# Attention: the running maximum read from the scores' own bank, softmax work on two tiles an instruction, no diagonal matrices

## The chip, the cores and the metric

One core of one Trainium2 chip runs the whole program. The metric is the time on the device in microseconds; each kernel is run several times and the median is compared. TensorE (PE) does matrix products, VectorE (DVE), ScalarE (ACT) and GpSimd (POOL) do element work, SyncE (SP) issues the transfers here. SBUF is the memory that all engines read; PSUM is the memory into which TensorE writes, in eight banks of 512 float32 columns.

## What is computed

A gated cross-attention block followed by a sparse feed-forward block, in float32:

```
# x (4, 256, 512), ctx (4, 1601, 512); 32 query heads, 8 key/value heads, head size 128
lat = layernorm(x)
kv  = concat([ctx, lat], axis=1)              # 1857 rows per batch
q   = rms_norm(lat @ Wq);  k = rms_norm(kv @ Wk);  v = kv @ Wv
p   = softmax(q @ k.T / sqrt(128))            # 4 query heads share one key/value head
x   = x + tanh(g_xattn) * ((p @ v) @ Wo)
x   = x + tanh(g_ffn) * ffn(layernorm(x))     # argmax of 32 picks the active rows
```

The change touches the attention loop alone: k, v, the scores, the softmax and the product with v.

## The kernel before

The program has four stages. `prepare` makes the queries, `attend` does the attention, `project` the product with Wo, `ffn` the rest. All products are made of three passes over values that are split into a rounded high part and the remaining low part (HI, LO), so that float32 accuracy comes from faster products.

`attend` runs 4 batches x 8 key/value heads = 32 rounds. A round has two halves (`h`), and a half 15 tiles (`t`): a tile is 128 rows of keys (65 in the last) against 512 query columns. For each tile: TensorE makes the scores in one of two banks of `pqk` ("qk"), ScalarE copies them to `sc` in SBUF, scaled by the key's norm `rk` ("copy", L729), VectorE takes the running maximum over tiles in `mx` ("max", L784 and L787). After 15 tiles TensorE transposes `mx` ("mt"), VectorE reduces it to 4 columns ("red", L790), multiplies an identity with them to get four diagonal matrices (`diag`, L767), and one product of ones with those spreads the maximum over all partitions in `pmax` ("mb", L647). Then, tile by tile again: subtract the maximum (VectorE, "sub", L798, already two tiles an instruction), exp in place (ScalarE, "exp", L732), round to the high part (ScalarE, "hi", L736), take the low part (VectorE, "lo", L802), add up the exps over tiles in `sm` (GpSimd, "sum", L855), and the product with V (TensorE, "pv", L656). The sums go the same way as the maximum: transposed ("dt"), reduced, inverted, made diagonal (L767), spread ("db", L670), multiplied in ("on", L820).

Beside this the K and V projections of the coming round (`pkv`, two banks used in turn; each chunk of 512 rows in three parts), the splitting of K and V, the transposes of V ("vt") and the norms of K ("kn" on TensorE into a bank `pss` of its own, "var" on VectorE L830, "pow" on GpSimd L861) are woven in.

The order of each engine's instructions is written by hand as numbers: every step has a place on an axis on which a tile is 1 and a round is 30, and each engine does its own steps in the order of their places. `LAG` is the distance from a tile's scores to its product with V. Who waits for whom is written out as semaphores: `wait_ge(sc_ok, ...)` and so on. What TensorE waits for before it overwrites a score bank is this line (L634):

```
pe.wait_ge(sc_ok, AHEAD + T - 1)      # the copy of the tile before the last
```

A bank of `pkv` is free when the step that used it before has been read (`wait_for_bank`).

## Time and profile before

| | before |
|---|---|
| median of 3 runs | 3674.18 us (3670.4 to 3681.19) |
| profiled execution, span | 3683.3 us; no other time is given for it |
| TensorE busy | 3184.8 us (86%), granted clock 0.952 |
| VectorE busy | 3152.2 us (86%) |
| ScalarE busy | 2121.6 us (58%) |
| GpSimd busy | 1668.6 us (45%) |
| attention loop | from about 260 to 3205 us |

Busy shares are over the whole span, with stages of different limits; the stages ahead of and behind the attention keep VectorE less busy, so a share of one stage says more. The profile is one execution on the one core.

### The profile page before, as it was taken

Reading aid. Unit: us, or ns where it says so; the run is one execution under the profiler, and the core shown is the slowest. Engines: PE = TensorE matmul, PEld = TensorE weight load, DVE = VectorE, ACT = ScalarE, POOL = GpSimd, SP = SyncE. Lnnn points to the kernel's source line nnn. Section 1 sums busy time; section 2 is a strip of 40 time slices with the busy share of each in tenths; the row PEclk is TensorE's granted clock in tenths of the full one; section 3 lists DMA queues with packets and bytes.
Section 4 is the critical chain, followed back from the end, with each engine's and each line's share of the span. In section 5 each row is a group of like instructions: output and inputs, shape, how many; then the busy total and the mean of one; then the engine's idle time right before and its main releaser. Section 6 shows DMA issues by size and latency. Waiting matters only on the chain. (4 is left out here: it accounts for less than half of the span.)

```text
span 3683.3 us, 52901 instructions
## 1 busy us (share of the span) xinstructions
PE 3184.8 (86%) x14138; PEld 2429.3 (66%) x14138; DVE 3152.2 (86%) x3890; ACT 2121.6 (58%) x3795; POOL 1668.6 (45%) x1175
## 2 busy tenths in 40 slices
PE   7978898889798988887989889878888888599699
PEld 5856666666476666665766666656666666277477
DVE  6856999999979999999799999988999999732666
ACT  3435666666656666666666666666666666431211
POOL 2322556555536555555455555544555555400000
PEclk9989999999999999999999999999999999799799
DMA  7870000000200000011000100110100000153400
GB/s 239 263 230 24 29 28 28 28 28 29 73 33 29 28 28 31 35 46 48 33 29 31 44 30 28 35 57 27 42 32 29 28 28 12 54 172 97 150 34 18
DMA packets 179314, 210.99 MB, mean 57 GB/s; under 512 B 10452, under 2 KB 125140, under 8 KB 174056
## 3 DMA queue, kind: packets, MB, share of 16 engines
q1 hardware_dynamic: 174408, 196.27, 16.2%
q0 software_dynamic: 2176, 8.39, 0.7%
q10 hardware_dynamic: 2592, 4.72, 0.4%
q8 instruction: 58, 0.95, 0.1%
q14 instruction: 80, 0.66, 0.1%
HBM read 140.14 MB, written 69.21 MB: 57 GB/s over the span
## 5 line engine op out<-in xcount | busy, mean ns | idle before, releaser
L855 POOL TENSOR_TENSOR att_sm<-att_sm,att_sc 128x512 f32<-128x512 f32 (+1 forms) x832 | 1305.6, 1569 | 545.9 <-ACT att_sc L732 490.1
L656 PE MATMUL att_ppv<-att_pr,att_V 128*128 128x512 f32 (+1 forms) x2880 | 907.6, 425 | 191.5 <-DVE att_pr L802 185.0
L732 ACT ACTIVATE att_sc<-att_sc 128x512 f32<-128x512 f32 (+1 forms) x960 | 611.9, 637 | 642.5 <-DVE att_sc L798 642.1
L802 DVE TENSOR_TENSOR att_pr<-att_sc,att_pr 128x512 fp32r<-128x512 f32 (+1 forms) x960 | 924.0, 964 | 0.7 <-ACT att_pr L736 0.7
L787 DVE TENSOR_TENSOR att_mx<-att_mx,att_sc 128x512 f32<-128x512 f32 (+1 forms) x832 | 883.6, 1062 | 41.2 <-ACT att_sc L729 38.5
L635 PE MATMUL att_pqk<-att_q,att_kT 128*128 128x512 f32 (+1 forms) x2880 | 881.3, 415 | 3.1 <-DVE att_kT L824 2.3
L605 PE MATMUL att_pkv<-att_ctxT,att_wkv 128*128 128x512 f32 (+1 forms) x3072 | 799.3, 384 | 75.9 <-DVE att_kT L824 71.8
L656 PEld LDWEIGHTS att_ppv<-att_pr,att_V 128*128 128x128 f32 (+1 forms) x2880 | 529.6, 198 | 421.4 <-DVE att_pr L802 318.0
L729 ACT ACTIVATE att_sc<-att_pqk,att_rk 128x512 f32<-128x512 f32 (+1 forms) x960 | 656.2, 684 | 129.1 <-PE att_pqk L635 123.8
L605 PEld LDWEIGHTS att_pkv<-att_ctxT,att_wkv 128*128 128x128 f32 x3072 | 564.0, 192 | 218.7 <-DVE att_kT L824 98.6
L736 ACT CAST att_pr<-att_sc 128x512 fp32r<-128x512 f32 (+1 forms) x960 | 599.3, 624 | 176.2 <-PE att_ppv L656 172.2
L798 DVE TENSOR_TENSOR att_sc<-att_sc,att_pmax 128x1024 f32<-128x1024 f32 (+1 forms) x512 | 584.6, 1142 | 58.1 <-PE att_pmax L647 58.1
L635 PEld LDWEIGHTS att_pqk<-att_q,att_kT 128*128 128x128 f32 (+1 forms) x2880 | 528.0, 189 | 143.1 <-issue 32.2
L861 POOL TENSOR_TENSOR att_rk<-att_var,att_mhalf 128x4 f32<-128x4 f32 (+1 forms) x128 | 174.4, 1363 | 562.0 <-DVE att_var L830 483.0
L852 POOL TENSOR_TENSOR att_sm<-att_sc 128x512 f32<-128x512 f32 x64 | 96.7, 1511 | 241.1 <-ACT att_sc L732 209.1
L1005 PE MATMUL out_po<-out_wo,out_o 128*128 128x512 f32 x768 | 180.2, 396 | 29.5 <-DVE out_wo L981 23.5
L291 PE MATMUL pre_pq<-pre_wq,pre_xT 128*128 128x512 f32 x768 | 195.2, 404 | 6.0 <-issue 6.0
L1005 PEld LDWEIGHTS out_po<-out_wo,out_o 128*128 128x128 f32 x768 | 146.2, 191 | 64.7 <-issue 21.9
L291 PEld LDWEIGHTS pre_pq<-pre_wq,pre_xT 128*128 128x128 f32 x768 | 141.6, 191 | 35.1 <-issue 6.4
L670 PE MATMUL att_pred<-att_diag,att_ones 128*128 128x512 f32 x128 | 84.9, 751 | 85.2 <-DVE att_diag L767 85.2
L237 POOL TENSOR_TENSOR pre_rq<-pre_ms,pre_mhalf 128x4 f32<-128x4 f32 x64 | 64.4, 1007 | 165.4 <-DVE pre_ms L349 165.4
L693 PEld LDWEIGHTS att_pss<-att_ones,att_sq 128*128 128x128 f32 (+1 forms) x960 | 122.1, 189 | 10.5 <-ACT att_sq L748 1.6
(129 smaller groups left out, 2697.2 us busy)
## 6 DMA issues: line engine op xcount, KB each, us to landing
q_scr<-pre_qT SPq DMA_DIRECT2D x128, 256.0 KB, 3.5
att_wkv<-kv_scr SPq DMA_DIRECT2D x32, 1024.0 KB, 4.8
att_q<-q_scr SPq DMA_DIRECT2D x64, 512.0 KB, 4.3
o_scr<-att_on SPq DMA_DIRECT2D x64, 256.0 KB, 2.0
out_oraw<-o_scr SPq DMA_DIRECT2D x64, 256.0 KB, 4.9
att_sc<-in_ctx SPq DMA_DIRECT2D x16, 768.0 KB, 4.6
pre_wq_raw<-in_L_xattn_Wq SPq DMA_DIRECT2D x8, 1024.0 KB, 6.8
kv_scr<-pre_kv SPq DMA_DIRECT2D x8, 1024.0 KB, 7.6
```

Source lines behind the costliest of these rows:

```text
L291: mm = pe.matmul(pq[:, t % 4], xT[:, xp, c, t * P:(t + 1) * P], wq[:, j, wp, c], start=(i == 0), stop=(i == 3 * KT - 1))
L605: mm = pe.matmul(bank, wkv[:, which, wp, t], ctxT[:, xp, t, a:z], start=(i == 0), stop=(i == len(terms) - 1))
L635: mm = pe.matmul(pqk[0:m, (h * NT + t) % 2], kT[:, kp, t * P:t * P + m], q[:, qp, h], start=(i == 0), stop=(i == 2))
L656: mm = pe.matmul(ppv[:], V[0:m, vp, t], pr[0:m, pp, (h * NT + t) % NP], start=(t == 0 and i == 0), stop=(t == NT - 1 and i == 2))
L729: act.activation(sc[0:m, s], pqk[0:m, s % 2], ACT.Copy, scale=rk[0:m, t:t + 1]).then_inc(sc_ok, 1)
L732: act.activation(sc[0:m, s], sc[0:m, s], ACT.Exp).then_inc(exp_ok, 1)
L736: act.copy(pr[0:m, HI, s % NP], sc[0:m, s]).then_inc(phi_ok, 1)
L787: dve.tensor_tensor(mx[0:m, h], mx[0:m, h], sc[0:m, s], ALU.max).then_inc(max_ok, 1)
L798: dve.tensor_tensor(sc[0:m, s:s + w], sc[0:m, s:s + w], pmax[0:m].unsqueeze(1).to_broadcast([m, w, HALF]), ALU.subtract).then_inc(sub_ok, w)
L802: dve.tensor_tensor(pr[0:m, LO, s % NP], sc[0:m, s], pr[0:m, HI, s % NP].bitcast(F32), ALU.subtract).then_inc(plo_ok, 1)
L855: pool.tensor_tensor(sm[0:m, h], sm[0:m, h], sc[0:m, s], ALU.add).then_inc(sum_ok, 1)
L1005: mm = pe.matmul(po[:, t], o[:, v % SL, op, h], wo[:, wp, e * HC + h], start=(e == 0 and h == 0 and p == 0), stop=(e == NE - 1 and h == HC ...
```

## The change

1. The running maximum (step "max") no longer reads `sc` but the scores' bank itself, and scales on the way: `scalar_tensor_tensor` of PSUM, the norm column and `mx`. It now has an instruction for the first tile too. It still follows ScalarE's copy, and TensorE's next scores but one wait for it (`max_ok`) in place of the copy (`sc_ok`).
2. "exp", "hi", "lo" and "sum" work on groups `GR` of two tiles; `pr` holds two groups of two in place of three tiles. GpSimd sums into two columns blocks (`sm[:, 0:2]`), with one "fold" at the end of a half. "sum" waits for the low parts of its own group (`plo_ok`) in place of the exps.
3. No `diag`: `spread` multiplies four columns, each broadcast to 128, with the identity, into quarters of the bank.
4. The norms of K use the banks of `pkv`, so a round has 16 uses of these in place of 12; `vraw` holds two chunks in place of all; the weights of K and of V are loaded apart.
5. `LAG` is 24 in place of 21.5, and the places of V's chunks and transposes, of "red", "dt" and of the loads move.

```diff
-    NP = 3
+    NP = 2
+    GR = [(t, min(t + 2, NT)) for t in range(0, NT, 2)]
-        vraw = sb("vraw", [P, NT * P])
+        vraw = sb("vraw", [P, 2, 512])
-        pr = sb("pr", [P, 2, NP, HALF], F32R)
-        sm = sb("sm", [P, NH, HALF])
+        pr = sb("pr", [P, 2, NP, 2, HALF], F32R)
+        sm = sb("sm", [P, 2, HALF])
-        diag = sb("diag", [P, 4, P])
-        pss = ps("pss", [P, 512])
...
-        LAG = 21.5
+        LAG = 24
-                if t % 2 == 0:
-                    steps += [(p + LAG - 4.3, "sub", h, t)]
-                steps += [(p + LAG - 3.14, "exp", h, t), (p + LAG - 2.3, "hi", h, t),
-                          (p + LAG - 1.63, "lo", h, t), (p + LAG, "pv", h, t)]
-                if t >= 1:
-                    steps += [(p + 1.18, "max", h, t), (p + LAG - 1.5, "sum", h, t)]
+            for g, (t, z) in enumerate(GR):
+                p = h * NT + t + LAG
+                steps += [(p - 4.3, "sub", h, g), (p - 3.2, "exp", h, g), (p - 2.4, "hi", h, g), (p - 1.6, "lo", h, g)]
+                if g >= 1:
+                    steps += [(p - 0.9, "sum", h, g)]
+            for t in range(NT):
+                steps += [(h * NT + t + 0.9, "max", h, t)]
...
-        for c, (k, v, vt) in enumerate(((-12.7, 1, 10.6), (-9, 4, 15.5), (-3.21, 6.63, 20.25), (-1.5, 11.35, 24.37))):
+        for c, (k, v, vt) in enumerate(((-12.7, 1, 12.6), (-9, 6, 16.6), (-3.21, 13, 20.6), (-1.5, 17.5, 24.6))):
...
-        steps += [(-17, "ldw", 0, 0)]
+        steps += [(-28, "ldwk", 0, 0), (-10.4, "ldwv", 0, 0)]
...
+                def spread(bank, col):
+                    for c in range(4):
+                        mm = pe.matmul(bank[:, c * P:(c + 1) * P], col[:, c:c + 1].to_broadcast([P, P]), ident[:],
+                                       start=True, stop=True)
+                    return mm
...
-                        pe.wait_ge(sc_ok, AHEAD + T - 1)
+                        pe.wait_ge(max_ok, AHEAD + T - 1)
...
-                        pe.wait_ge(diag_ok, AHEAD + u + 1)
+                        pe.wait_ge(red_ok, AHEAD + u + 1)
                         pe.wait_ge(sub_ok, AHEAD + NT * u)
-                        pe.matmul(pmax[:], ones[:], diag[:].rearrange("p c n -> p (c n)"),
-                                  start=True, stop=True).then_inc(mb_ps, 1)
+                        spread(pmax, red).then_inc(mb_ps, 1)
...
+                        wait_for_bank(n, dn, before, xb)
                         pe.wait_ge(ksq_ok, AHEAD + NC * n + t + 1)
-                            mm = pe.matmul(pss[0:rows(i), i:i + 1], sq[:, t % 2, (i % 4) * P:(i % 4) * P + rows(i)],
+                            mm = pe.matmul(pkv[0:rows(i), BANK["kn", t], i:i + 1], sq[:, t % 2, (i % 4) * P:(i % 4) * P + rows(i)],
...
-                            dve.tensor_tensor(mx[0:m, h], mx[0:m, h], sc[0:m, s], ALU.max).then_inc(max_ok, 1)
+                            dve.scalar_tensor_tensor(out=mx[0:m, h], in0=pqk[0:m, s % 2], scalar=rk[0:m, t:t + 1],
+                                                     in1=mx[0:m, h], op0=ALU.mult, op1=ALU.max).then_inc(max_ok, 1)
...
-                        diagonal(red).then_inc(diag_ok, 1)
...
-                        dve.wait_ge(phi_ok, AHEAD + T + 1)
-                        dve.tensor_tensor(pr[0:m, LO, s % NP], sc[0:m, s], pr[0:m, HI, s % NP].bitcast(F32),
-                                          ALU.subtract).then_inc(plo_ok, 1)
+                        dve.wait_ge(phi_ok, AHEAD + grouped(n, h, t))
+                        dve.tensor_tensor(pr[0:m, LO, t % NP, 0:w], sc[0:m, h, i:i + w], pr[0:m, HI, t % NP, 0:w].bitcast(F32),
+                                          ALU.subtract).then_inc(plo_ok, w)
...
-                        pool.wait_ge(exp_ok, AHEAD + T + 1)
+                        pool.wait_ge(plo_ok, AHEAD + grouped(n, h, t))
...
+                            pool.wait_ge(sum_ok, AHEAD + grouped(n, h, t - 1))
+                            pool.tensor_tensor(sm[0:m, 0:w], sm[0:m, 0:w], sc[0:m, h, i:i + w], ALU.add).then_inc(sum_ok, w)
+                    elif what == "fold":
+                        pool.wait_ge(sum_ok, AHEAD + NT * (u + 1))
+                        pool.tensor_tensor(sm[:, 0], sm[:, 0], sm[:, 1], ALU.add).then_inc(fold_ok, 1)
```

Three places show what the numbers do to the order in the loop over rounds. The first is TensorE around the spread of the first half's maximum (`att_pmax`), from the transposes of V's second chunk on; `att_pkv<-att_ctxT,att_wkv` are the projections, 512 columns a full chunk, 322 the last. Before:

```order
L633 REGISTER_ALU
L635 MATMUL att_pqk<-att_q,att_kT 128x512 [waits att_sc_ok]
L635 MATMUL att_pqk<-att_q,att_kT 128x512 x2
L620 ISA [waits att_vraw_ok]
L605 MATMUL att_pkv<-att_ctxT,att_wkv 128x512 [waits att_w_in]
L605 MATMUL att_pkv<-att_ctxT,att_wkv 128x512 x3
L650 REGISTER_ALU
L656 MATMUL att_ppv<-att_pr,att_V 128x512 [waits att_plo_ok]
L656 MATMUL att_ppv<-att_pr,att_V 128x512 x2
L645 REGISTER_ALU
L646 ISA [waits att_diag_ok]
L647 MATMUL att_pmax<-att_diag,att_ones 128x512 [waits att_sub_ok]
```

Now:

```order
L635 ISA [waits att_vraw_ok]
L611 MATMUL att_pkv<-att_ctxT,att_wkv 128x512 [waits att_wk_in]
L611 MATMUL att_pkv<-att_ctxT,att_wkv 128x512 x3
L611 MATMUL att_pkv<-att_ctxT,att_wkv 128x322 [waits att_wv_in,att_vlo_ok]
L611 MATMUL att_pkv<-att_ctxT,att_wkv 128x322 x3
L664 REGISTER_ALU
L670 MATMUL att_ppv<-att_pr,att_V 128x512 [waits att_plo_ok]
L670 MATMUL att_ppv<-att_pr,att_V 128x512 x2
L660 REGISTER_ALU
L661 REGISTER_ALU [waits att_red_ok]
L619 MATMUL att_pmax<-att_ident,att_red 128x128 [waits att_sub_ok]
L619 MATMUL att_pmax<-att_ident,att_red 128x128 x3
```

The last chunk of V (322 columns) now stands ahead of the spread and waits for `att_vlo_ok`, the low half of the V transpose that TensorE has made just before.

The second is VectorE at the same place: the low parts (`att_pr`), the maximum (`att_mx`), the low half of V, the last subtraction of a half (`att_sc`, 65 rows). Before:

```order
L801 REGISTER_ALU
L802 TENSOR_TENSOR att_pr<-att_sc,att_pr 128x512 [waits att_phi_ok]
L798 TENSOR_TENSOR att_sc<-att_sc,att_pmax 65x512
L789 REGISTER_ALU
L790 TENSOR_REDUCE att_red<-att_pred 128x4 [waits att_mt_ps]
L767 TENSOR_TENSOR att_diag<-att_ident,att_red 128x512 [waits att_db_ps,att_red_ok]
L801 REGISTER_ALU
L802 TENSOR_TENSOR att_pr<-att_sc,att_pr 128x512 [waits att_phi_ok]
L836 REGISTER_ALU
L837 TENSOR_TENSOR att_V<-att_pkv,att_V 128x512 [waits att_vhi_ok]
```

Now:

```order
L816 REGISTER_ALU
L817 TENSOR_TENSOR att_pr<-att_sc,att_pr 128x1024 [waits att_phi_ok]
L794 REGISTER_ALU
L795 REGISTER_ALU [waits att_sc_ok]
L800 SCALAR_TENSOR_TENSOR att_mx<-att_pqk,att_rk,att_mx 128x512 [waits att_max_ok]
L845 REGISTER_ALU
L846 TENSOR_TENSOR att_V<-att_pkv,att_V 128x512 [waits att_vhi_ok]
L811 TENSOR_TENSOR att_sc<-att_sc,att_pmax 65x512
```

The last subtraction stood ahead of the reduction of the next maximum, two places ahead of V's low half; now it stands behind the next maximum and V's low half, and the spread above waits for it.

The third is GpSimd where a half's sums end; L861 and L863 before, L875 and L877 now, are the powers for the K norms. Before:

```order
L855 TENSOR_TENSOR att_sm<-att_sm,att_sc 128x512 [waits att_sum_ok,att_exp_ok]
L858 REGISTER_ALU
L860 REGISTER_ALU [waits att_var_ok]
L861 TENSOR_TENSOR att_rk<-att_var,att_mhalf 128x2 [waits att_sc_ok]
L863 TENSOR_TENSOR att_rk<-att_var,att_mhalf 65x1
L849 REGISTER_ALU
L855 TENSOR_TENSOR att_sm<-att_sm,att_sc 65x512 [waits att_sum_ok,att_exp_ok]
L849 REGISTER_ALU
L851 ISA [waits att_exp_ok]
L852 TENSOR_TENSOR att_sm<-att_sc 128x512 [waits att_dt_ps]
```

Now:

```order
L874 REGISTER_ALU [waits att_var_ok]
L875 TENSOR_TENSOR att_rk<-att_var,att_mhalf 128x2 [waits att_max_ok]
L877 TENSOR_TENSOR att_rk<-att_var,att_mhalf 65x1
L860 REGISTER_ALU
L866 TENSOR_TENSOR att_sm<-att_sm,att_sc 128x1024 [waits att_sum_ok,att_plo_ok]
L860 REGISTER_ALU
L866 TENSOR_TENSOR att_sm<-att_sm,att_sc 65x512 [waits att_sum_ok,att_plo_ok]
L868 ISA
L869 TENSOR_TENSOR att_sm<-att_sm 128x512 [waits att_sum_ok]
L860 REGISTER_ALU
L862 REGISTER_ALU [waits att_plo_ok]
L863 TENSOR_TENSOR att_sm<-att_sc 128x1024 [waits att_dt_ps]
```

A sum takes two tiles, waits for `att_plo_ok` in place of `att_exp_ok`, and an instruction that folds the two blocks stands behind the last.

## Rows read from the trace of the kernel before

**Rows 1.** Busy time by stretch: four rounds in a batch, and its first round.

```profile
core 0: us, PE busy (x) PEld busy (x) DVE busy (x) ACT busy (x) POOL busy (x), PEclk, DMA share, GB/s
1126.00:1474.00 348.00, 309.36 (x1381) 236.27 (x1380) 335.58 (x396) 235.67 (x431) 200.85 (x133) 0.97 0.09 30
...
1027.00:1060.00 33.00, 32.52 (x155) 26.05 (x156) 16.73 (x28) 18.03 (x31) 2.63 (x3) 1.00 0.21 74
```

**Rows 2.** Timeline of the transfer queue: two loads of K and V weights, four rounds apart.

```profile
1126.03 0.35 SPq L567 DMA_DIRECT2D att_wkv<-kv_scr  x1
...
1474.32 0.35 SPq L567 DMA_DIRECT2D att_wkv<-kv_scr  x1
```

**Rows 3.** Waits from 500 to 3000 us: who waited for whom, total, times, longest.

```profile
ACT att_sc L732 <- DVE att_sc L798: 554.2, 315, 3.4
...
POOL att_rk L861 <- DVE att_var L830: 392.3, 84, 10.3
...
PE att_ppv L656 <- DVE att_pr L802: 147.3, 165, 2.4
```

**Rows 4.** Groups of VectorE's instructions by shape, 1126 to 1474 us: busy, mean ns.

```profile
L802 DVE TENSOR_TENSOR att_pr<-att_sc,att_pr 128x512 fp32r<-128x512 f32 x112 | 106.4, 950 | 0.0
L787 DVE TENSOR_TENSOR att_mx<-att_mx,att_sc 128x512 f32<-128x512 f32 x96 | 103.9, 1083 | 0.5
...
L767 DVE TENSOR_TENSOR att_diag<-att_ident,att_rden 128x512 f32<-128x512 f32 x8 | 12.7, 1591 | 0.6
L787 DVE TENSOR_TENSOR att_mx<-att_mx,att_sc 65x512 f32<-65x512 f32 x8 | 9.8, 1224 | 0.0
```

**Rows 5.** Timeline of VectorE and of GpSimd, 1543 to 1552 us: start, duration.

```profile
1543.83 1.21 DVE L798 TENSOR_TENSOR att_sc<-att_sc,att_pmax 128x1024 f32<-128x1024 f32 x1
1544.96 0.68 DVE L802 TENSOR_TENSOR att_pr<-att_sc,att_pr 128x512 fp32r<-128x512 f32 x1
1545.56 1.77 DVE L787 TENSOR_TENSOR att_mx<-att_mx,att_sc 128x512 f32<-128x512 f32 x1
1547.26 1.78 DVE L802 TENSOR_TENSOR att_pr<-att_sc,att_pr 128x512 fp32r<-128x512 f32 x1
...
1545.21 6.70 POOL L855 TENSOR_TENSOR att_sm<-att_sm,att_sc 128x512 f32<-128x512 f32 x4
```

**Rows 6.** Single lines over the whole run: duration ns min/median/max.

```profile
L358 DVE SCALAR_TENSOR_TENSOR pre_qT<-pre_ptr,pre_wcol,pre_qT x64: 743/745/751, 46.7 to 247.4; 128x512 fp32r<-128x512 f32 x64
...
L977 DVE TENSOR_TENSOR out_o<-out_oraw,out_o x32: 1217/1224/1227, 3213.0 to 3391.6; 128x1024 fp32r<-128x1024 f32 x32
...
L855 POOL TENSOR_TENSOR att_sm<-att_sm,att_sc x832: 1261/1558/3655, 337.7 to 3195.2; 128x512 f32<-128x512 f32 x154, 65x512 f32<-65x512 f32 x13
```

**Rows 7.** Timeline of TensorE in the first round of a batch.

```profile
1031.07 0.95 PE L693 MATMUL att_pss<-att_ones,att_sq 128*128 128x1 f32 x8
1031.88 0.94 PE L635 MATMUL att_pqk<-att_q,att_kT 128*128 128x512 f32 x3
...
1039.04 0.85 PE L635 MATMUL att_pqk<-att_q,att_kT 128*128 128x512 f32 x3
1039.73 1.10 PE L605 MATMUL att_pkv<-att_ctxT,att_wkv 128*128 128x512 f32 x4
1040.67 0.87 PE L635 MATMUL att_pqk<-att_q,att_kT 128*128 128x512 f32 x3
...
1055.19 1.02 PE L647 MATMUL att_pmax<-att_diag,att_ones 128*128 128x512 f32 x2
1055.65 1.25 PE L635 MATMUL att_pqk<-att_q,att_kT 128*128 128x512 f32 x3
...
1083.02 0.76 PE L605 MATMUL att_pkv<-att_ctxT,att_wkv 128*128 128x322 f32 x4
1083.62 0.87 PE L635 MATMUL att_pqk<-att_q,att_kT 128*65 128x512 f32 x3
```

**Rows 8.** Timeline of TensorE and ScalarE: a tile's scores and their copy.

```profile
1504.01 0.85 PE L635 MATMUL att_pqk<-att_q,att_kT 128*128 128x512 f32 x3
...
1505.03 0.69 ACT L729 ACTIVATE att_sc<-att_pqk,att_rk 128x512 f32<-128x512 f32 x1 [0.54 <-PE att_pqk L635]
```

More of the change, by code:

```diff
@@ L470, in attend @@
                    for d, what in ((0, "xt"), (0.26, "xhi"), (0.6, "xlo"))]
-        loads = [(12.89, "ldw", 0, 0), (12.89 + .1, "ldlat", 0, 0)]
-        loads += [(z - 1 + LAG - 1.5 + .1, "ldx", 0, i) for i, (a, z) in enumerate(XP)]
+        loads = [(2, "ldwk", 0, 0), (19.6, "ldwv", 0, 0), (19.7, "ldlat", 0, 0)]
+        loads += [(z - 1 + LAG - 0.5, "ldx", 0, i) for i, (a, z) in enumerate(XP)]
         def window(*parts):
@@ L483, in attend @@
         in_boundary = [x for x in loads if x[0] >= UT]
-        start_early = [x for x in early if x[1] != "ldw"]
+        start_early = [x for x in early if x[1] not in ("ldwk", "ldwv")]
         START = window((0, -2 * UT, loads), (0, 0, context), (0, UT - 3.33, start_early))
@@ L491, in attend @@
         TAIL = window((-1, -UT, late))
-        USES = [(dn, what, c) for dn, what, h, c in MIDDLE if what in ("k", "v", "vt") and h == 0]
+        USES = [(dn, what, c) for dn, what, h, c in MIDDLE if what in ("k", "v", "vt", "kn") and h == 0]
         BANK = {(what, c): i % 2 for i, (_, what, c) in enumerate(USES)}
-        assert len(USES) == 3 * NC
+        assert len(USES) == 4 * NC
         BANK.update({("xt", i): i % 2 for i in range(CT)})
@@ L531, in rounds, with grouped, maxima @@
             run(B * KVH, TAIL, [], last=True)
-        def sums(n, h, t):
-            return n * UT + (h * NT + max(t, 1) + 1)
+        def grouped(n, h, g):
+            return tiles(n, h, GR[g][1] - 1)
+        def maxima(u, t):
+            return u * NM + t + 1
         def tiles(n, h, t):
@@ L638, in step @@
                     elif what == "mt":
-                        pe.wait_ge(max_ok, AHEAD + (NT - 1) * (u + 1))
+                        pe.wait_ge(max_ok, AHEAD + maxima(u, NT - 1))
                         pe.wait_ge(on_ok, AHEAD + u - 1)
@@ L665, in step @@
                         for c in range(4):
-                            mm = pe.transpose(pred[:, c * P:(c + 1) * P], sm[:, h, c * P:(c + 1) * P], ident[:])
+                            mm = pe.transpose(pred[:, c * P:(c + 1) * P], sm[:, 0, c * P:(c + 1) * P], ident[:])
                         mm.then_inc(dt_ps, 1)
                     elif what == "db":
-                        pe.wait_ge(ddiag_ok, AHEAD + u + 1)
-                        pe.matmul(pred[:], ones[:], diag[:].rearrange("p c n -> p (c n)"),
-                                  start=True, stop=True).then_inc(db_ps, 1)
+                        pe.wait_ge(rden_ok, AHEAD + u + 1)
+                        spread(pred, rden).then_inc(db_ps, 1)
                     elif what == "xt":
@@ L807, in step @@
                         dve.wait_ge(den_ok, AHEAD + u + 1)
+                        dve.wait_ge(db_ps, AHEAD + u)
                         dve.reciprocal(rden[:], den[:]).then_inc(rden_ok, 1)
-                        dve.wait_ge(rden_ok, AHEAD + u + 1)
-                        if last and h == 1:
-                            dve.wait_ge(db_ps, AHEAD + u)
-                        else:
-                            dve.wait_ge(mb_ps, AHEAD + u + 2)
-                        diagonal(rden).then_inc(ddiag_ok, 1)
                     elif what == "on":
```

117 lines of the change are left out of this document (62 added, 55 removed).

## The prediction

> **What bounds the kernel now.** I read the busy time of each engine by stretch first. In four whole rounds of the attention loop VectorE is busy 335.6 of 348 us (96%) and TensorE 309.4 (89%), ScalarE 235.7, GpSimd 200.9 [rows 1]. A round (one head of keys and values, two halves of 15 tiles) is the distance between loads of its weights: four of them lie between 1126.03 and 1474.32, so 87.1 us each [rows 2]. In the round that opens a batch, where no softmax work of an earlier round is left, TensorE is busy 32.5 of 33 us and VectorE half of it [rows 1]: that is what the loop looks like when TensorE sets the pace.
>
> The waits say the same. Over 2500 us ScalarE's exp waits 554 us for VectorE's subtraction and TensorE's product with V waits 147 us for VectorE's low halves [rows 3]. VectorE is the bound.
>
> The groups of VectorE's instructions by shape show why it is so full. The 512-column low-half subtraction (L802) has a mean of 950 ns, the maximum (L787) 1083 [rows 4], though both take 0.68 us when nothing is in the way. The timeline shows what is: during 6.70 us of four back-to-back sums on GpSimd, instructions with both inputs in SBUF take 1.77 and 1.78 us, one after the other, that is 0.68 plus a wait of 1.1, and the subtraction of the maximum, one input of which is PSUM, takes its usual 1.21 [rows 5]. So what stretches VectorE is GpSimd's sums, and only for instructions with two SBUF inputs.
>
> **VectorE, part by part, for one round** (a quarter of the counts of [rows 4]).
> - Stretching now: L802 112 x (0.950 - 0.68) = 30.2; L787 96 x (1.083 - 0.68) = 38.7 and 8 x (1.224 - 0.68) = 4.4; the diagonal of the reciprocals 8 x (1.591 - 0.68) = 7.3. Sum 80.6 over four rounds, 20.2 a round.
> - The maximum reads PSUM and SBUF. No row shows it on this operand pair with GpSimd at work; the nearest are the scaled subtraction of the first stage (L358, PSUM and SBUF, 745 ns [rows 6]) and L798, which does not stretch. I take 0.745, so 28 x 0.065 more, and two more instructions a round (a tile now costs one each, also the first) at 0.60 from start to start [rows 5]: +3.0. If it stretched as L787 does now: +11 more.
> - The diagonals go: four a round, 0.61 each unstretched: -2.4.
> - Low halves in pairs: 1.22 us for 1024 columns (L977 [rows 6]), about 1.13 from start to start as L798 has it [rows 5], against 2 x 0.60: 14 x 0.07 = -1.0.
> - The low halves' own stretching: a sum now waits for the low halves of its own pair, so it starts when VectorE has just left the port, and the next low half stands about two tiles (5 us) later, behind two maxima and a subtraction that read PSUM. A sum of two tiles costs at most 2 x 1.26 = 2.5 us [rows 6]. It is over by then, unless an rsqrt (L861) is queued before it. I keep 3 of the 20.2.
> Busy 335.6 / 4 = 83.9, less 20.2, less 2.4, less 1.0, plus 3.0, plus 3: 66 us a round. VectorE stops being the bound.
>
> **TensorE, for one round.** Three 512-column products take 0.70 from start to start, four take 0.94, four of 322 columns 0.60 [rows 7]. 30 scores and 30 products with V: 60 x 0.70 = 42.0; K and V projections 18 x 0.94 + 6 x 0.60 = 20.5; norms 3 x 0.81 + 0.5, four spreads at 0.46, and eight groups of four transposes at no more than that each: 8.4. That is 70.9. A spread becomes four products of 128 columns in place of one of 512, each with its own weight load: the same columns, so I cost it at nothing; at worst it doubles, +1.8 a round. This is at the full clock; the granted mean is 0.97 in [rows 1], and half-speed pieces stretch products while TensorE is the bound: 73.
>
> TensorE's work isn't spread evenly: where K or V parts stand beside a tile it has 2.3 us a tile, elsewhere 1.4, and there VectorE's 1.8 (half of 1.13 + 1.13 + 2 x 0.67) decides. With two score banks neither can run more than about a tile ahead. Adding the busier engine over ten stretches of three tiles gives 73, with the clock 75.
>
> **New waits.** The score bank was free after ScalarE's copy; now the next scores but one wait for VectorE's maximum. From the start of the scores to the copy is 1.02 us [rows 8], copy 0.69, maximum 0.75, handoffs 0.1 each: 2.6 us before VectorE can do anything that stands behind this maximum, 3.3 with that next instruction. At five places TensorE waits for just that, after work of only 0.70 + 0.94 us; the first two stand in the order rows, the others follow from the places given to the steps. (1) V's last chunk waits for the low half of the V transpose, one maximum behind: 1.6. (2) The spread of the maximum waits for the last subtraction of the half before, which the larger LAG put behind one more maximum: 1.5. (3) The norm products, now in the projections' banks: chunk 3 waits for the raw V behind a copy, 1.0. (4) K's third chunk waits for a V low half that follows the norms: 1.0. (5) Smaller ones at the third V transpose and the first norm, 0.6 together. Sum 5.7, of which I let 1.2 be hidden where VectorE decides anyway: 4.5. Round: 75 + 4.5 = 79.5.
>
> ScalarE does the same columns in fewer instructions and GpSimd's sums keep their columns. I cost both at nothing: at 59 and 50 us a round [rows 1] they hide behind TensorE's 73, and without that cover a gain of ScalarE would still be none.
>
> **Sum.** 87.1 - 79.5 = 7.6 us a round. In each of four batches about 40 us already run at TensorE's pace (33 of them in [rows 1]), so 30 rounds count: 228. The pipeline is 2.5 tiles longer and drains four times, 2.5 x 79.5 / 30 = 6.6 us each if nothing fills it, 0 if all; I take 12. 3683.3 - 228 + 12 = 3467. The page gives no time for the profiled execution beside its span; the span is 9 us above the median of the three runs, 3674. So 3458; I say 3455.
>
> **Rivals.**
> - *The new waits are hidden* (20%). For it: now VectorE idles only 4%, so this queue order has been tolerant. Then a round is 73 to 75: 3683 - 30 x 13 + 5 - 9, about 3290 (3260 to 3320).
> - *The maximum becomes the pace* (20%). For it: TensorE can't go two tiles ahead without it, and each late low half on VectorE is passed on. The waits double to 10 and a round is 84.5: 3683 - 30 x 2.6 + 26 - 9 = 3620; more likely half way, 3540.
> - *Longer sums block the low halves* (5%), the one that ends slower. Place: GpSimd's queue behind L861, which waits 392 us over 2500 for the variances [rows 3], so sums pile up and run back to back. Price: the wait of 1.1 us beside a sum of 1.26 to 1.56 becomes about 2.2 beside two tiles; 16 low halves a round x 2.2 = 35, VectorE 63 + 35 = 98, a round 102: 3683 + 30 x 15 - 9, over 4100. It decides from a mean wait of (83.9 - 63) / 16 = 1.3 us, where VectorE is back where it is now. Against it: the sum's new wait for its own low half, and only one instruction in four, not two, can be hit. The Trainium skill (SBUF — State Buffer, Who interferes with whom) says that the pair of ports is held for a whole GpSimd instruction and the other engine blocks fully, and that one SBUF input never contends. The first half speaks against this change, whose sums are twice as long, and leads to this rival; the second is what L798 shows in [rows 5].
> - *Nothing changes* (3%): TensorE, 89% busy, is already nearly the pace. Against it: 32.5 of 33 us when it is.
>
> **How the numbers follow.** The likeliest case (52%) is 3400 to 3520. To hold 8 in 10 the range goes from the hidden waits to the maximum's pace: 3290 to 3600. A measurement can tell 0.3% (11 us) from no change. The three cases that are faster hold 0.92, no change 0.03, the blocked low halves 0.05.
>
> **What would show it.** Mean of the maximum about 0.75 us and never over 1; low halves of 1024 columns near 1.3; no stretch over 2.5. VectorE 80 to 84% busy in a round, TensorE over 90%; a round 79.5 us. TensorE waiting some 5 us a round, for the V low half, the last subtraction and the maximum. I am wrong if low halves show a mean above 2 us, if the maximum stretches, or if TensorE's wait for the maximum is the largest group.

## The result

The changed kernel takes 3753.8 us (median of 4 runs, 3746.1 to 3759.1) against 3672.3 for the kernel before in the same comparison (3668.0 to 3681.2): a ratio of 1.021, with a 95% interval of 1.0183 to 1.0238. It is 2.1% slower, where 6% faster was forecast, and lies outside the range.

The page of the changed kernel gives the engines over the whole span of 3751.9 us (busy us, share, instructions).

```profile
PE 3214.2 (86%) x14906; PEld 2532.9 (68%) x14906; DVE 2568.1 (68%) x3378; ACT 2044.9 (55%) x2899; POOL 1350.9 (36%) x791
```

VectorE did 584 us less work (3152 before), as foretold, and it bought nothing: TensorE is busy for about as long as before (3214 against 3185 us) in a longer span. The groups of VectorE and GpSimd by shape, 500 to 3000 us (busy, mean ns, idle time before), answer to [rows 4]:

```profile
L800 DVE SCALAR_TENSOR_TENSOR att_mx<-att_pqk,att_rk,att_mx 128x512 f32<-128x512 f32 x701 | 523.2, 746 | 259.9 <-ACT att_sc L742 256.5 <-issue 0.8
L817 DVE TENSOR_TENSOR att_pr<-att_sc,att_pr 128x1024 fp32r<-128x1024 f32 x377 | 473.1, 1255 | 101.6 <-ACT att_pr L753 101.5
...
L866 POOL TENSOR_TENSOR att_sm<-att_sm,att_sc 128x1024 f32<-128x1024 f32 x269 | 643.2, 2391 | 576.5 <-DVE att_pr L817 575.9 <-issue 0.6
```

The maximum costs 746 ns with GpSimd at work (1083 before), a low half of two tiles 1255 (950 for one before). The stretching is nearly gone: the maximum's longest instruction takes 754 ns, and single low halves still reach 2.94 us. What came in its place shows in the waits of the same 2500 us (engine, what it waited for, total, times, longest), which answer to [rows 3]:

```profile
ACT att_sc L742 <- PE att_pqk L650: 746.7, 484, 6.9
...
PE att_pkv L611 <- DVE att_V L846: 93.0, 51, 3.1
...
PE att_ppv L670 <- ACT att_oraw L757: 71.6, 51, 1.7
...
PE att_pmax L619 <- DVE att_sc L811: 46.2, 27, 3.9
PE att_pqk L650 <- DVE att_mx L800: 41.2, 80, 0.7
PE att_pkv L706 <- ACT att_vraw L770: 37.3, 27, 1.4
PE att_pkv L720 <- DVE att_kT L833: 31.2, 27, 1.3
```

ScalarE now waits 747 us for TensorE: TensorE is the pace. And TensorE, on which everything hangs, waits 320 us in six groups, none of them large, for VectorE and ScalarE, which have time to spare. There are about 27 rounds in the stretch, so a group with 27 times is one wait a round, 51 two, 80 three. TensorE had waited in the kernel before as well, 147 us for the low halves in [rows 3], and in the same view of it these:

```profile
PE att_pred L670 <- DVE att_diag L767: 68.3, 49, 3.7
PE att_pkv L605 <- DVE att_kT L824: 61.9, 48, 1.8
```

In the 2500 us it was idle for 312 us then (2188 busy) and is idle for 349 now (2151 busy): old waits went and new ones came, a few more than before.

One round, by the same two marks as in [rows 2] (start, duration), is 1350.81 - 1261.85 = 88.96 us, against 87.1 before and 79.5 forecast (the 28 rounds that lie within a batch have a mean of 89.0); under the marks the busy times in it (PE, PEld, DVE, ACT, POOL, then the granted clock), which answer to [rows 1]:

```profile
1261.85 0.35 SPq L571 DMA_DIRECT2D att_wkv<-kv_scr  x1
...
1350.81 0.34 SPq L571 DMA_DIRECT2D att_wkv<-kv_scr  x1
```

```profile
1261.85:1350.81 88.96, 76.76 (x371) 61.17 (x370) 65.13 (x83) 56.73 (x82) 39.62 (x22) 0.98 0.08 29
```

All waits of TensorE of half a microsecond or more in that round, from its timeline (in brackets the idle time before the group), with a few rows on what a spread costs:

```profile
1264.20 0.66 PE L720 MATMUL att_pkv<-att_ident,att_vraw 128*128 128x128 f32 x4 [1.14 <-DVE att_kT L833]
...
1274.12 0.95 PE L670 MATMUL att_ppv<-att_pr,att_V 128*128 128x512 f32 x3 [1.39 <-ACT att_oraw L757]
...
1277.62 0.96 PE L650 MATMUL att_pqk<-att_q,att_kT 128*128 128x512 f32 x3 [0.53 <-DVE att_mx L800]
...
1282.65 1.20 PE L611 MATMUL att_pkv<-att_ctxT,att_wkv 128*128 128x512 f32 x4 [1.45 <-DVE att_V L846]
...
1302.33 1.16 PE L619 MATMUL att_pmax<-att_ident,att_red 128*128 128x128 f32 x8 [1.44 <-DVE att_sc L811]
1303.24 0.94 PE L670 MATMUL att_ppv<-att_pr,att_V 128*128 128x512 f32 x3
1304.02 0.86 PE L650 MATMUL att_pqk<-att_q,att_kT 128*128 128x512 f32 x3
1306.27 0.72 PE L706 MATMUL att_pkv<-att_ones,att_sq 128*128 128x1 f32 x6 [1.39 <-ACT att_vraw L770]
...
1311.08 0.96 PE L650 MATMUL att_pqk<-att_q,att_kT 128*128 128x512 f32 x3 [0.50 <-DVE att_mx L800]
...
1316.08 0.86 PE L670 MATMUL att_ppv<-att_pr,att_V 65*128 65x512 f32 x3
1316.77 0.90 PE L650 MATMUL att_pqk<-att_q,att_kT 128*128 128x512 f32 x3
1319.13 0.96 PE L670 MATMUL att_ppv<-att_pr,att_V 128*128 128x512 f32 x3 [1.46 <-ACT att_oraw L757]
...
1325.37 0.97 PE L650 MATMUL att_pqk<-att_q,att_kT 128*128 128x512 f32 x3 [0.66 <-DVE att_mx L800]
...
1341.45 0.86 PE L611 MATMUL att_pkv<-att_ctxT,att_wkv 128*128 128x322 f32 x4 [2.19 <-DVE att_V L846]
```

Their sum is 12.2 us; the rest of the round, 76.8, is TensorE's work. The wait of 1.46 shows how one arises. ScalarE's timeline for it:

```profile
1317.92 0.69 ACT L742 ACTIVATE att_sc<-att_pqk,att_rk 128x512 f32<-128x512 f32 x1 [0.65 <-PE att_pqk L650]
1318.50 0.58 ACT L757 COPY att_oraw<-att_ppv 128x512 f32<-128x512 f32 x1
```

The scores start at 1316.77. ScalarE's queue has their copy next (1317.92), and only behind it the copy of the finished output, "oraw" (1318.50), though the last product of the output, started at 1316.08, had ended 1.5 us before; TensorE's next product with V needs that bank and starts at 1319.13. So a step that is ready is held by a step that stands ahead of it in the handwritten order and waits for TensorE's newest work. Seven of the ten waits, 10.5 us together, have this form: scores, their copy, perhaps their maximum, then the late step. The other three, 1.7 us, are TensorE's waits for the maximum itself. There the copy had ended 0.9 to 3.2 us before the maximum started, and what stood ahead of it was other work in VectorE's queue, each time with a subtraction of two tiles (1.2 us) in it. The pairs add to the longest wait too, 2.19. VectorE's timeline for it:

```profile
1338.92 1.21 DVE L817 TENSOR_TENSOR att_pr<-att_sc,att_pr 128x1024 fp32r<-128x1024 f32 x1
1340.06 0.74 DVE L800 SCALAR_TENSOR_TENSOR att_mx<-att_pqk,att_rk,att_mx 128x512 f32<-128x512 f32 x1
1340.72 0.68 DVE L846 TENSOR_TENSOR att_V<-att_pkv,att_V 128x512 fp32r<-128x512 f32 x1
```

The copy ended at 1339.53; the low half of two tiles held the maximum, and so V's low half, 0.5 us longer.

### The profile page after: what moved, and what is told of

It is laid out like the page before. It is cut to its first block and busy times, and to the rows that moved or that the text cites. A ratio compares the mean times of both kernels' runs of the same rounds, so it can differ in the third digit from the quotient of the medians.

```text
span 3751.9 us, 52506 instructions
## 1 busy us (share of the span) xinstructions
PE 3214.2 (86%) x14906; PEld 2532.9 (68%) x14906; DVE 2568.1 (68%) x3378; ACT 2044.9 (55%) x2899; POOL 1350.9 (36%) x791
## 5 line engine op out<-in xcount | busy, mean ns | idle before, releaser
L866 POOL TENSOR_TENSOR att_sm<-att_sm,att_sc 128x1024 f32<-128x1024 f32 (+1 forms) x384 | 847.9, 2208 | 784.9 <-DVE att_pr L817 784.3
L800 DVE SCALAR_TENSOR_TENSOR att_mx<-att_pqk,att_rk,att_mx 128x512 f32<-128x512 f32 (+1 forms) x896 | 668.6, 746 | 321.5 <-ACT att_sc L742 316.7
L817 DVE TENSOR_TENSOR att_pr<-att_sc,att_pr 128x1024 fp32r<-128x1024 f32 (+1 forms) x512 | 624.0, 1219 | 122.5 <-ACT att_pr L753 122.1
L753 ACT CAST att_pr<-att_sc 128x1024 fp32r<-128x1024 f32 (+1 forms) x512 | 509.3, 995 | 101.4 <-PE att_ppv L670 100.6
L747 ACT ACTIVATE att_sc<-att_sc 128x1024 f32<-128x1024 f32 (+1 forms) x512 | 512.9, 1002 | 32.2 <-DVE att_sc L811 32.0
L875 POOL TENSOR_TENSOR att_rk<-att_var,att_mhalf 128x4 f32<-128x4 f32 (+1 forms) x128 | 146.5, 1145 | 531.0 <-DVE att_var L839 411.9
L863 POOL TENSOR_TENSOR att_sm<-att_sc 128x1024 f32<-128x1024 f32 x64 | 153.1, 2393 | 418.5 <-PE att_pred L680 394.8
L833 DVE TENSOR_TENSOR att_kT<-att_pkv,att_kT 128x512 fp32r<-128x512 f32 (+1 forms) x128 | 82.1, 642 | 154.7 <-ACT att_sq L765 154.1
L706 PEld LDWEIGHTS att_pkv<-att_ones,att_sq 128*128 128x128 f32 (+1 forms) x960 | 121.4, 189 | 69.0 <-ACT att_vraw L770 58.0
L706 PE MATMUL att_pkv<-att_ones,att_sq 128*128 128x1 f32 (+1 forms) x960 | 115.3, 240 | 45.4 <-ACT att_vraw L770 44.1
```

Of the source, the lines that this page charges most:

```text
L747: act.activation(sc[0:m, h, i:i + z - a], sc[0:m, h, i:i + z - a], ACT.Exp).then_inc(exp_ok, z - a)
L753: act.copy(pr[0:m, HI, t % NP, 0:z - a], sc[0:m, h, i:i + z - a]).then_inc(phi_ok, z - a)
L800: dve.scalar_tensor_tensor(out=mx[0:m, h], in0=pqk[0:m, s % 2], scalar=rk[0:m, t:t + 1], in1=mx[0:m, h], op0=ALU.mult, op1=ALU.max).then_i ...
L817: dve.tensor_tensor(pr[0:m, LO, t % NP, 0:w], sc[0:m, h, i:i + w], pr[0:m, HI, t % NP, 0:w].bitcast(F32), ALU.subtract).then_inc(plo_ok, w)
L866: pool.tensor_tensor(sm[0:m, 0:w], sm[0:m, 0:w], sc[0:m, h, i:i + w], ALU.add).then_inc(sum_ok, w)
```

## The experiments

Theory A: TensorE is the pace, and each of these waits is lost time of its own, so taking one away gives its size in each of some 32 rounds. Theory B: the score bank, held until VectorE's maximum, is what sets the pace. Theory C: the sums of two tiles hurt the low halves after all. The median follows each label; "before" is the kernel before in the same comparison. The changed kernel itself was timed only in the first comparison, and the kernel before has medians from 3672 to 3682 us in the five, so a difference from the changed kernel's 3753.8 is good to some 10 us. Of the edits only the parts of lines that matter are shown, and `...` marks what is left out between them.

**One place moved: 3697.5.** The copy of the output goes ahead of the scores' copy.

```diff
-(f - 0.6, "oraw", h, 0)
+(f - 0.65, "oraw", h, 0)
```

> The changed kernel with one number changed: ScalarE's copy of the finished output bank (step oraw) stands at f - 0.65 in place of f - 0.6, which puts it ahead of the copy of the next scores instead of behind it. Theory A (TensorE now sets the pace, and its waits at a few places of the hand-written order add up to the loss): its wait for oraw, 1.39 and 1.46 us in the two halves of the round at 1262 us, falls to some 0.3 each, so 2.2 us a round and 60 to 75 us of the whole, about 3685. Theory B (the score bank, held until the maximum, is the pace): the time saved here is spent waiting for the maximum again, under 15 us gained.

Ratio to before 1.0042 (1.0025 to 1.0059): 56 us less than the changed kernel. The wait for "oraw" falls from 71.6 to 6.8 us over the 2500, but its neighbours grew: over the same stretch TensorE waits

```profile
PE att_pqk L650 <- DVE att_mx L800: 56.9, 83, 1.1
PE att_pkv L720 <- DVE att_kT L833: 52.7, 50, 1.3
```

in place of 41.2 and 31.2. A wait that goes gives a part of its size to the others: here 37 of the 65 us. That the time still fell by 56 us has a second reason, shown behind the last run.

**Another place moved: 3647.2.** The low half of V's transpose stands ahead of a maximum.

```diff
-(vt + 1.64, "vtlo", 0, c)
+(vt + 1.25, "vtlo", 0, c)
```

> The changed kernel with one number changed: the low half of a V transpose stands 1.25 behind the transpose in place of 1.64, so ahead of the maximum of a tile whose scores TensorE has just made, and ahead of the norms. Theory A: the waits of TensorE for att_V, 2.19 us at V's last chunk and 1.45 at K's third, fall below 0.5 each, some 3 us a round and 80 to 95 us of the whole, about 3665. Theory B: under 20 us.

Ratio 0.9905 (0.9885 to 0.9924), 107 us less, somewhat more than expected. But the waits did not fall below 0.5 us each: over the 2500 us TensorE still waits

```profile
PE att_pkv L611 <- DVE att_V L846: 54.2, 47, 2.5
```

in place of 93.0, and the other groups stay within 4 us. That is some 1.4 us a round, where the rounds became 3.5 us shorter. The number agrees with theory A for a reason that is only in part theory A's.

**A third score bank: 3701.2.** TensorE waits for the maximum of the tile three before, not two (the bank `pss` that the change gave up makes room).

```diff
-pqk = ps("pqk", [P, 2, 512])
+pqk = ps("pqk", [P, 3, 512])
...
-pe.wait_ge(max_ok, AHEAD + T - 1)
+pe.wait_ge(max_ok, AHEAD + T - 2)
```

> The changed kernel with a third bank for the scores, so that TensorE waits for the maximum of the tile three back instead of two. Theory A: only its direct waits for the maximum go, 0.5 + 0.5 + 0.66 us in the round at 1262 us, 1.7 a round, 40 to 55 us of the whole, about 3705. Theory B: the loop falls to TensorE's own work, 75 us a round, over 300 us gained, 3450 or less.

Ratio 1.0051 (1.0034 to 1.0068), 53 us less, about the size of the three waits for the maximum (1.7 us a round). The wait for the maximum is gone (1.3 us over the 2500 in place of 41.2). The others stay about as they were (the V low half 94.6, "oraw" 75.0); only TensorE's wait for the low halves grew, from 13.8 to 30.4. Theory B falls.

**The diagonals put back: 3915.2.** The changed kernel with `diag` and the single product of 512 columns.

> The changed kernel with the diagonal matrices and the single product with ones brought back (four more VectorE instructions a round). Theory A: a spread by four small products takes 0.91 us on TensorE from start to start against 0.46 before, so four a round give back 1.8 us, up to 55 us of the whole, less what the wait for the diagonal costs before the product: 3695 to 3740. Theory B: no change within 10 us, or slower by VectorE's added 2.4 us a round.

Ratio 1.0637 (1.0616 to 1.0659), 161 us more, 5 us a round, where 14 to 59 less were expected. VectorE has 4 x 0.61 us more work in a round, and 23.8 us of idle time to do it in (89.0 - 65.1); but the diagonals stand in its queue ahead of steps that TensorE waits for. The V low half is waited for 131.5 us here, 93.0 in the changed kernel; the maximum 68.2 (41.2), the last subtraction 56.6 (46.2):

```profile
PE att_pkv L612 <- DVE att_V L862: 131.5, 48, 4.4
```

Waiting is 3.4 us a round of the loss; the rest is TensorE's own busy time, at a lower granted clock (the table behind the last run).

**Four places moved: 3492.4.** "oraw" and "vtlo" as above, the spread of the maximum later, the norms of K's last chunk one tile later.

```diff
-(e + 3, "mb", h, 0)
+(e + 3.8, "mb", h, 0)
...
-(k + 3.5, "kn", 0, c), (k + 3.6, "var", 0, c), (k + 3.7, "pow", 0, c)
+(k + 3.5 + (c == 3), "kn", 0, c), (k + 3.6 + (c == 3), "var", 0, c), (k + 3.7 + (c == 3), "pow", 0, c)
```

> The changed kernel with four numbers of the order changed: oraw and the V low half as in the two runs before, the spread of the maximum at e + 3.8 in place of e + 3 (behind the last subtraction that it waits for), and the norms of K's last chunk one tile later (behind the copy of the raw V). Theory A (TensorE is the pace and its waits add): the four waits go, 2.2 + 3.3 + 1.4 + 1.4 = 8.3 us of a round of 88.9, so 80.6 and about 3500 in all. Theory B (something else takes their place, VectorE's or ScalarE's queue): the single gains of 56 and 107 us are not exceeded by more than 50, about 3550 to 3600.

Ratio 0.9502 (0.9457 to 0.9546). Four numbers in the order, with no operation changed, are worth 261 us, about what was expected (3500).

**All waits treated: 3340.5.** The former, the third score bank, and two more places.

```diff
-(-9, 6, 16.6)
+(-9, 6, 15.6)
...
-(k + 0.9, "khi", 0, c)
+(k + 0.7, "khi", 0, c)
```

> The same with three more: a third bank for the scores, the transposes of V's second chunk one tile earlier (so that V's last chunk finds its bank free), and the splitting of K a fifth of a tile earlier, ahead of a score copy. Theory A: 1.7 us of waits for the maximum, 1.5 for V's low half and 1.1 for K's low half go too, a round of 76.5 and about 3380. Theory B: with TensorE that dense, VectorE and ScalarE come late at new places and half of it is lost, about 3450.

Ratio 0.9088 (0.9046 to 0.9131), 413 us less than the changed kernel. The marks of a round, and the busy times in it (PE, PEld, DVE, ACT, POOL, granted clock, DMA share, GB/s):

```profile
1079.83 0.36 SPq L571 DMA_DIRECT2D att_wkv<-kv_scr  x1
...
1156.42 0.35 SPq L571 DMA_DIRECT2D att_wkv<-kv_scr  x1
```

```profile
1079.83:1156.42 76.59, 74.37 (x371) 60.28 (x370) 66.62 (x84) 56.29 (x81) 41.12 (x21) 1.00 0.10 34
```

TensorE is idle for 2.2 us of 76.6 here, at the full clock, so its work is 74.4 us. VectorE's is 66.6, as the prediction had it (66).

**The sums wait for the exps: 3772.0.** The changed kernel, with GpSimd's sums earlier and no longer behind the low halves of their own pair.

```diff
-steps += [(p - 0.9, "sum", h, g)]
+steps += [(p - 2.3, "sum", h, g)]
...
-pool.wait_ge(plo_ok, AHEAD + grouped(n, h, t))
+pool.wait_ge(exp_ok, AHEAD + grouped(n, h, t))
```

> The changed kernel, but GpSimd's sum of a pair waits for the pair's exps (as before the change), not for its low parts, and stands 1.4 earlier. If the sum's new wait is what keeps the two engines off the shared port, the low parts of 1024 columns stretch again, from 1.22 us to 2 or more in the mean, some 8 us more of VectorE a round. Theory A: VectorE has 20 us a round to spare, but TensorE's waits lie behind VectorE's queue, so a part shows: 30 to 100 us slower than the changed kernel. Theory B (the port doesn't matter any more): within 10 us.

Ratio 1.0278 (1.0230 to 1.0326), against 1.0183 to 1.0238 for the changed kernel: the intervals overlap a little. The low halves of two tiles take 1453 ns on average in place of 1255. So the sums' new wait and their later place, changed here together, do keep them apart, but by the medians only some 18 us hang on it (25 by the ratios), which is not clear of the noise. In the changed kernel the sums hardly hurt the low halves (1255 ns, 1.22 us unstretched), so theory C falls as the cause.

**The maximum alone, in the old order: 3514.8.** The kernel before; only the running maximum reads the score bank (15 a half), and TensorE waits for `max_ok`. One tile an instruction, diagonals and all places as before.

```diff
-if t >= 1:
-    steps += [(p + 1.18, "max", h, t), (p + LAG - 1.5, "sum", h, t)]
+if t >= 1:
+    steps += [(p + LAG - 1.5, "sum", h, t)]
+steps += [(p + 1.18, "max", h, t)]
...
-pe.wait_ge(sc_ok, AHEAD + T - 1)
+pe.wait_ge(max_ok, AHEAD + T - 1)
```

> The kernel before with one part of the change alone: the maximum reads the scores' bank, scaled on the way, in the old order with LAG 21.5, single tiles and diagonals; TensorE waits for it. Theory A: VectorE loses the maximum's stretching (11 us a round) and gains 3, and the old places hold fewer waits for TensorE, so a round of about 80 to 82 and 3490 to 3540. Theory B (holding the bank until the maximum costs more than it gives): slower than before, above 3700.

Ratio 0.9571 (0.9527 to 0.9616): 4.3% faster. The maximum does not stretch, the low halves (both inputs from SBUF) still do; VectorE's groups, 500 to 3000 us:

```profile
L804 DVE TENSOR_TENSOR att_pr<-att_sc,att_pr 128x512 fp32r<-128x512 f32 x826 | 821.8, 996 | 1.1 <-ACT att_pr L737 1.0
L788 DVE SCALAR_TENSOR_TENSOR att_mx<-att_pqk,att_rk,att_mx 128x512 f32<-128x512 f32 x764 | 565.9, 741 | 32.1 <-ACT att_sc L730 31.7
```

**The treated kernel with the diagonals: 3460.1.** The kernel of 3340.5 with `diag` back, to see what they cost where the places are clear.

> The re-placed kernel (seven changes of order and the third score bank, 3340 us, a round of 76.6) with the diagonal matrices and the single product brought back. Theory A (in the changed kernel the diagonals cost 161 us because VectorE's two more steps stand right where TensorE waits for it): with those places cleared TensorE's 1.8 us a round for four spreads comes back and some of VectorE's steps still show, so between 20 us faster and 60 us slower than 3340. Theory C (the diagonal itself is slow for TensorE or VectorE wherever it stands): again 100 to 160 us slower, 3440 to 3500.

Ratio 0.9418 (0.9402 to 0.9435), 120 us more than without. Again most of it is waiting: the V low half is waited for 72.8 us over the 2500 (13.5 without), the last subtraction 19.9 (8.4).

```profile
PE att_pkv L612 <- DVE att_V L862: 72.8, 52, 2.3
```

**The spread alone, in the old order: 3607.5.** The kernel before, with four products of 128 columns and no diagonals.

> The kernel before with one part of the change alone: no diagonals, four products against the identity spread the maximum and the sums. VectorE, the pace there, loses four instructions of 0.61 a round and 1.8 us of stretching; TensorE gains up to 1.8 us that it has to spare. Theory A: 4.2 us of a round of 87.1, so 100 to 135 us faster, about 3550 to 3580. Theory C (TensorE's small products with a broadcast column are dear): under 50 us faster.

Ratio 0.9821 (0.9800 to 0.9841): 1.8% faster, 67 us, where 100 to 135 us were expected. The diagonals' 2.4 us a round plus their stretching are gone, but VectorE's maximum (1096 ns) and low halves (957) stretch on, and TensorE still waits 170 us for the low halves.

**Both in the old order: 3479.8.** The kernel before with the maximum and the spread, all but the pairs and the places rewritten for them.

> The kernel before with two of the change's three parts: the maximum reads the scores' own bank for all 15 tiles, and the spreads take four products of 128 columns without diagonal matrices. The softmax work stays on one tile an instruction, and every place of the order stays as before. The maximum alone gave 3515 (161 less than before), the spread alone 67 less. If the loss of the changed kernel lies in the third part, the pairs with the places that were rewritten for them, the two gains add up: 3515 - 67 = about 3450, no more than 3480, and the third part costs some 300 us. Rival: the two parts hurt each other, since the spread now waits for a subtraction that stands behind maxima which hold the score banks; then it ends well above the maximum alone, near the changed kernel's 3754 or at least above 3560.

Ratio 0.9456 (0.9440 to 0.9472): 202 us less than before (3682.1). The two gains nearly add up (163 + 68 = 231 by the medians). So all that the changed kernel has beyond this one costs some 274 us: the pairs with `LAG` 24 and the new places, and with them the norms in the projections' banks, the smaller `vraw` and the split loads. No run tried these one by one; what the treated kernel shows is that with other places and a third score bank all of them together run in 3340.5 us. TensorE's largest waits here, 500 to 3000 us:

```profile
PE att_pqk L642 <- DVE att_mx L792: 167.9, 244, 2.4
PE att_ppv L662 <- DVE att_pr L806: 15.7, 21, 1.9
```

The six groups of the changed kernel are not there: in the old order the late steps stood at other places. There is another, for the maximum (longer still, 221 us, with the maximum alone), 5.5 us a round, since VectorE (223 of 245 us busy in three rounds) is nearly full.

**The other two places alone: 3636.6.** The changed kernel with "mb", "kn", "var" and "pow" moved as above, and nothing else.

> The changed kernel with two places moved alone: the spread of the maximum at e + 3.8 (was 3), and the norms of K's last chunk with their variance and rsqrt one tile later. In its trace TensorE waits 1.44 us a round for the subtraction ahead of the spread and 1.39 for the raw V ahead of the norms, together 2.83. If each wait removed gives its size in each of some 32 rounds: 90 less, about 3663; and by the difference of the kernel with all four places (262 less) and the two tried alone (56 and 107): 99 less. Rival: TensorE's waits are passed on and not saved, since VectorE with its maxima is the true pace; then less than 40 of it is seen, above 3710.

Ratio 0.9879 (0.9862 to 0.9895), 117 us less, where 90 to 99 were expected: the two waits' 2.83 us x 32 is 90. Alone, the three parts of the four-places kernel give 56, 107 and 117, together 280, and 261 at once. By the marks of the weight loads, the 28 rounds that lie within a batch take 91 us less in the profiled executions (2491 to 2400), 3.3 a round; the three distances from one batch to the next take 19 us less (363.0 to 343.5).

**What a gain is made of.** Five rounds in a row within a batch, from mark to mark (busy times as above):

```profile
1171.34:1621.05 449.71, 389.77 (x1847) 310.21 (x1846) 325.83 (x415) 283.64 (x402) 198.89 (x106) 0.97 0.08 29
1085.38:1517.49 432.11, 380.33 (x1847) 302.20 (x1846) 325.19 (x416) 284.05 (x401) 203.26 (x105) 0.99 0.09 30
1079.83:1462.67 382.84, 371.74 (x1846) 301.32 (x1845) 333.00 (x416) 281.32 (x401) 205.62 (x105) 1.00 0.10 34
```

These are the changed kernel, the one with the V low half moved, and the treated one. A fifth of such rows, in us a round (a batch's early rounds are shorter, which is why 89.9 lies above the mean of 89.0):

| kernel | round | TensorE busy | TensorE idle | granted clock |
|---|---|---|---|---|
| before | 87.3 | 77.7 | 9.5 | 0.96 |
| changed | 89.9 | 78.0 | 12.0 | 0.97 |
| "oraw" moved | 87.3 | 76.4 | 10.9 | 0.99 |
| V low half moved | 86.4 | 76.1 | 10.4 | 0.99 |
| other two places | 87.0 | 78.0 | 9.0 | 0.96 |
| diagonals back | 95.6 | 80.2 | 15.4 | 0.94 |
| treated | 76.6 | 74.3 | 2.2 | 1.00 |

TensorE does the same products in all but the first and the sixth, so its busy time differs there mostly by the clock. The change made the loop slower by idle time, 12.0 in place of 9.5 us, not by work. Of the 13.4 us that the treated kernel gains on the changed one, 9.8 are idle time and 3.6 busy time. Moving the V low half gives 3.5 us, of which 1.6 are idle time and 1.9 busy time; the other two places give 2.9, all of it idle time. So theory A holds for what sets the pace, but its rule "a wait taken away gives its size" leaves out the clock, and the waits' sizes alone do not foretell a gain. Which waits bring the clock down was not tried.

## Why the prediction was wrong

**VectorE** was right: 66 us forecast, 65.1 busy in the round of the changed kernel and 66.6 in the treated one. The maximum at 0.745 us was right (0.746), so was the end of the stretching, nearly.

**The step that failed is "New waits".** It counted five places with 5.7 us, 4.5 after hiding. The round above has ten waits with 12.2:

| wait in the round | forecast | measured |
|---|---|---|
| V's last chunk for the V low half | 1.6 | 2.19 |
| spread for the last subtraction | 1.5 | 1.44 |
| norms of chunk 3 for raw V | 1.0 | 1.39 |
| K's third chunk for a V low half | 1.0 | 1.45 |
| third V transpose and first norm; a V transpose for K's low half | 0.6 | 1.14 |
| product with V for "oraw", twice | none | 2.85 |
| scores for the maximum, three times | none | 1.69 |

The method was sound where it was used, a chain of scores, copy and maximum ahead of the late step, set against TensorE's work meanwhile. But I walked only the places that the diff names, and left out of the chain that VectorE's low halves and subtractions of two tiles, 1.2 us each, can stand in it. "oraw" keeps its place at f - 0.6; what moved is `LAG`, from 21.5 to 24. With a fraction of 0.5 the scores and the products with V of two halves stood half a tile apart; with a whole number the copy of a tile's scores (x + 0.39) falls just ahead of "oraw" (x + 0.4). The run with 0.65 in place of 0.6 shows that it is this. And I let 1.2 us be hidden "where VectorE decides anyway": the trace shows it deciding only at the three short waits for the maximum, and the waits that I had listed came to 7.6 us, not 4.5.

**TensorE's own work** was undersized as well: 70.9 forecast at the full clock, 74.4 measured in the treated kernel. Two costs stand in no group's own row. The group behind a small product starts its next one after 0.78 us in place of 0.70 (1303.24 to 1304.02 above), behind each of 16 spreads, transposes and norms: 1.3 us. And a spread takes 0.91 us (1302.33 to 1303.24), where I took 0.46 from the product with the diagonals: 1.8 us for four. That makes 3.1 of the 3.5. That row of [rows 7] misled: the product has 0.46 us from start to start, but the group behind it shows 1.25 us in place of 0.86, so it cost 0.85. The edit itself is thus nearly free, as costed, and the floor under both kernels was higher; the 0.4 us that are left have no row. With the clock (0.98 in this round) 76.8 stand against my 75.

Sum: 76.8 + 12.2 = 89.0, against 75 + 4.5. Of the 9.5 us missing in a round 7.7 are waits and 1.8 work. My 75 already held some 2 us for tiles at which VectorE decides, which the trace shows as the three waits for the maximum (1.69); with these counted among the waits, as in the table, some 5.6 of the 9.5 are waits and 3.8 are TensorE's own time (76.8 against 73). Over 32 rounds (89.0 - 87.1) x 32 = 61 us more than before, and the span is 69 longer.

**The signs.** None of the three signs by which I would have been wrong came: no mean of the low halves above 2 us, no stretched maximum, and TensorE's wait for the maximum only the fourth group. All three looked at VectorE and the score bank. What did show it were numbers of the forecast itself: VectorE 73% busy in the round (forecast 80 to 84), TensorE 86% (over 90), and 12.2 us of waits (some 5).

**The rivals.** "The maximum becomes the pace" (3620) came nearest by number, and that is luck: a third bank takes this wait away and gives only 53 us. "Longer sums block the low halves" did not happen in the changed kernel (1.26 us on average, against 1.22 [rows 6] where nothing is in the way). The condition on it, a sum that starts just behind the low half of its own pair, carried it: without that wait, and with the sums earlier, the mean is 1.45. In the treated kernel one low half in a half does meet a sum; timelines of VectorE and of GpSimd:

```profile
1094.21 2.94 DVE L817 TENSOR_TENSOR att_pr<-att_sc,att_pr 65x512 fp32r<-65x512 f32 x1
```

```profile
1094.20 2.40 POOL L866 TENSOR_TENSOR att_sm<-att_sm,att_sc 128x1024 f32<-128x1024 f32 x1
```

The two start together, and the low half, 0.68 us by itself [rows 5], ends 0.55 us after the sum does: it was held for 2.26 us, nearly the whole 2.40 of the sum. This agrees with the rule that the prediction weighed (the Trainium skill, SBUF — State Buffer, Who interferes with whom): the other engine is blocked for a whole GpSimd instruction. The rule fits this row, and it decided nothing here. "The new waits are hidden" (3290) is roughly what the treated kernel reaches, 3340, once they are taken away.

What stays open: the other two places gave 117 us where their waits add up to 90. The rounds within the batches account for 91 and the passages between batches for 19, but why the passages gained that much was not taken apart. Open too is what each further part of the change (pairs, `LAG`, places, banks, loads) costs by itself.

## What to carry to other kernels

When the bound moves from one engine to another, the old engine's slack no longer covers the order of the queues: walk every step of every queue that the new bound waits for, not only those that the diff moves, and ask for each what stands ahead of it and when that can run. A constant that shifts two interleaved streams against each other by half a tile changes all their neighbours at once. And a part of a change whose mechanism works (4.3% and 1.8% alone here) can be hidden by another part's order, so time the parts one by one, and fix the order before judging a part. Signs of being wrong belong on the new bound, not only on the engine that was relieved.

## What the hardware showed that I had not expected

- A product's cost need not stand in its own row: the 512-column product with the diagonals shows 0.46 us from start to start, and the other 0.39 in the next group's duration (1.25 against 0.86) [rows 7].
- VectorE's maximum, with one of its inputs from PSUM, never stretched beside GpSimd: in four kernels the longest of its 896 instructions took 754 ns (the means are 741 to 746), with GpSimd's sums at work beside it.
- Behind TensorE's longest wait of the round (2.19 us) the granted clock fell from 2.4 to 1.2 GHz for a few microseconds, and the products took nearly twice as long, in TensorE's timeline of the changed kernel:

```profile
1342.97 1.91 PE L619 MATMUL att_pmax<-att_ident,att_red 128*128 128x128 f32 x8
1344.54 1.63 PE L650 MATMUL att_pqk<-att_q,att_kT 128*128 128x512 f32 x3
```

The busy times and the granted clock (0.50) of this piece:

```profile
1342.90:1345.90 3.00, 3.00 (x12) 2.70 (x11) 0.00 (x0) 0.00 (x0) 0.00 (x0) 0.50 0.00 0
```

From start to start the spread takes 1.57 us here in place of 0.91. In the treated kernel's round, which has no wait over 0.7 us, the clock is 1.00. So a wait can cost more than its length. With that wait made shorter (the V low half moved) five rounds have 0.99 in place of 0.97, and TensorE is busy for 1.9 us a round less. The other two places took away more idle time (3.0 against 1.6 us a round) and left the clock low (0.96).
